# Sparse and linear attention on one core: three reciprocals on ScalarE, GpSimd masks in two steps, a hand-written ending per engine

## The chip, the cores and the metric

The kernel runs on one core of one Trainium2 chip. The metric is the device time of one launch, in microseconds (us). A core has five engines that run their own instruction streams and wait for each other by semaphores: TensorE (PE), VectorE (DVE), ScalarE (ACT), GpSimd (POOL) and SyncE (SP), which here only issues DMAs.

## The reference, cut to what matters

32 batches of 256 tokens with 128 channels, 16 heads of 8 channels. For each batch and head, scores of 256 x 256 are made, the 12 largest of each row are kept (`topk = int(256 * 0.05)`), and a sparse softmax over them is mixed with a linear attention over all keys:

```python
def _L0_attn_ref(x, Wqkv, bqkv, q_gamma, q_beta, k_gamma, k_beta, alpha, Wproj, bproj):
    ...
    q = _layernorm(q, q_gamma, q_beta)
    k = _layernorm(k, k_gamma, k_beta)
    scores = jnp.einsum('bhnd,bhmd->bhnm', q, k) / jnp.sqrt(jnp.float32(D))
    aw = jax.nn.softmax(scores, axis=-1)
    topk = max(1, int(N * TOPK_RATIO))
    kth = jax.lax.top_k(aw, topk)[0][..., -1:]
    mask = (aw >= kth).astype(aw.dtype)
    aws = aw * mask
    aws = aws / (aws.sum(-1, keepdims=True) + 1e-08)
    o_s = jnp.einsum('bhnm,bhmd->bhnd', aws, v)
    qf = jax.nn.softmax(q, axis=-1)
    kf = jax.nn.softmax(k, axis=-1)
    kv = jnp.einsum('bhnd,bhne->bhde', kf, v)
    z = jnp.einsum('bhnd,bhd->bhn', qf, kf.sum(axis=2))
    o_l = jnp.einsum('bhnd,bhde->bhne', qf, kv) / (z[..., None] + 1e-06)
    o = (a * o_s + (1.0 - a) * o_l).transpose(0, 2, 1, 3).reshape(B, N, C)
    return o @ Wproj.T + bproj
    ...
xn = _layernorm(x, axis=-1)
x = x + _L0_attn_ref(xn, ...) + _L0_ffn_ref(xn, ...)
```

The second branch picks one of eight 128 x 128 matrices and applies it to `xn`.

## The kernel before

A batch is cut into 8 units (`UNITS`) of two heads. A unit has four tiles (`TILES`) of 128 queries x 256 keys. All engines run `body(it)` for `it` from -2 to B + 1; in an iteration each engine steps through the units `u_` = 0 to 7, in an order written out by hand, and the batches are staggered: scores of batch `it`, input and normalisation of batches `it + 1` and `it + 2`, output of `it - 1` and `it - 2`. No scheduler is involved.

A tile goes this way. PE makes the scores (`score_ps`, two buffers). DVE takes the 8 largest (`largest`, tile `top`). POOL subtracts the row maximum (`drop`). ACT takes the exponential (`e`, with the row sum in `z`) and that of the 8 largest (`e8`). One unit later DVE removes those 8 (`remove`, MATCH_REPLACE8, tile `rest`) and takes the next 8 (`following`, tile `next`), of which one is the twelfth largest value, the threshold. Two units after the scores the mask `below` is made: POOL compares 24 of a batch's 32 tiles with the threshold (`POOL_TILES` tiles of each unit), ACT makes the other 8 with a Relu of the difference. Four units after the scores PE transposes `e` and adds the mask times -2^40 (`turn`, into `turn_ps`), ACT clips that to `kept` with a Relu, and PE multiplies it with the values (`product`, one quad of four heads at a time, into `pv_ps`). ACT copies each quad to `oT`, PE turns the four quads back with a transpose against `gather` (`sums`), and ACT copies numerators and denominators to `sums_sb`.

Three sets of reciprocals are taken on DVE, each of 128 x 32 numbers, once a batch, inside `extra`: `lin_z` (denominator of the linear attention) in unit 4, `k_rec` (softmax of k) in unit 6, and `den` (denominator of the sparse attention, to which POOL first adds 1e-8 times `z` in two instructions) in unit 7. POOL then multiplies by them (`lin`, `k_feat`, `o_sparse`). ACT normalises the input (`xn`, two instructions of 128 x 128 in unit 5). The output of a batch is put together in `early` of units 1 and 3, two iterations later: transposes of `o_sparse` and `lin`, an ACT copy `osT`, then the residual `x_res`, the chosen matrix, a bias and the projection. The last two batches go through the same code, in iterations 32 and 33, where most branches are empty.

## Time and profile before

| | us |
|---|---|
| median of three runs | 1214.25 (1212.27 to 1215.47) |
| the profiled execution, its own time | 1203.79 |
| its span, first to last instruction | 1202.0 |
| busy in the span | PE 951.5, DVE 1164.2, ACT 1094.4, POOL 1090.9 |

Busy time of an engine is the union of its instructions, so two that overlap count once. "Mean ns" is the duration of one instruction; since neighbours overlap, the step from one start to the next is often shorter. "idle before" is the gap in front of an instruction, and behind the arrow stands who ended it.

### The profile page before, as it was taken

Reading aid. Unit: us, or ns where it says so; the run is one execution under the profiler, and the core shown is the slowest. Engines: PE = TensorE matmul, PEld = TensorE weight load, DVE = VectorE, ACT = ScalarE, POOL = GpSimd, SP = SyncE. Lnnn points to the kernel's source line nnn. Section 1 sums busy time; section 2 is a strip of 40 time slices with the busy share of each in tenths; the row PEclk is TensorE's granted clock in tenths of the full one; section 3 lists DMA queues with packets and bytes.
Section 4 is the critical chain, followed back from the end, with each engine's and each line's share of the span. In section 5 each row is a group of like instructions: output and inputs, shape, how many; then the busy total and the mean of one; then the engine's idle time right before and its main releaser. Section 6 shows DMA issues by size and latency. Waiting matters only on the chain.

```text
span 1202.0 us, 34514 instructions
## 1 busy us (share of the span) xinstructions
PE 951.5 (79%) x9028; PEld 647.2 (54%) x9028; DVE 1164.2 (97%) x4448; ACT 1094.4 (91%) x3566; POOL 1090.9 (91%) x1691
## 2 busy tenths in 40 slices
PE   4578788887788788788788787888888788787786
PEld 1355555555555555555555555555555555555554
DVE  6999999999999999999999999999999999999993
ACT  3699999999999999999999998999999999999984
POOL 5699999999999999999999999999999999999974
PEclk9999999999999999999999999999999999999998
DMA  3122222122222122222122222122222121222210
GB/s 102 41 63 67 86 84 72 49 70 65 85 85 80 42 75 59 85 85 85 38 74 59 85 85 84 40 73 59 85 85 85 46 67 58 85 81 80 58 34 14
DMA packets 165126, 82.77 MB, mean 69 GB/s; under 512 B 7737, under 2 KB 164927, under 8 KB 164930
## 3 DMA queue, kind: packets, MB, share of 16 engines
q1 hardware_dynamic: 164658, 80.43, 23.4%
q8 instruction: 74, 1.21, 0.4%
q14 instruction: 122, 1.00, 0.3%
q10 hardware_dynamic: 272, 0.13, 0.0%
HBM read 42.78 MB, written 37.75 MB: 67 GB/s over the span
## 4 chain that ended last, share of the span: by engine, by line
ACT 33%; DVE 28%; issue 19%; PE 9%; POOL 8%; DVEq 2%; DMA 0%; POOLq 0%; ACTq 0%
ACT e L821 19%; DVE rest L646 11%; DVE top L639 10%; POOL below L440 6%; ACT kept L788 4%; DVE next L652 4%; PE pv_ps L964 3%; PE work_ps L1030 2%; ACT below L834 2%; DVEq L75 2%; ACT e L826 1%; PE turn_ps L943 1%; ACT osT L793 1%; ACT oT L843 1%; ACT xnT L882 1%
## 5 line engine op out<-in xcount | busy, mean ns | idle before, releaser
L440 POOL TENSOR_SCALAR below<-e,next 128x256 bf16<-128x256 f32 x768 | 695.8, 922 | 0.0
L821 ACT ACTIVATE e<-score_ps,drop 128x256 f32<-128x256 f32 x1024 | 475.1, 493 | 42.8 <-POOL drop L410 39.7
L646 DVE MATCH_REPLACE8 rest<-e 128x256 f32<-128x256 f32 x1024 | 416.7, 411 | 0.1
L652 DVE MAX8 next<-rest 128x8 f32<-128x256 f32 x1024 | 409.4, 413 | 0.3
L943 PE MATMUL turn_ps<-ident,e 128*128 128x128 f32 x2048 | 388.4, 284 | 15.7 <-ACT kept L788 15.7
L944 PE MATMUL turn_ps<-minus_huge,below 128*128 128x128 bf16 x2048 | 367.8, 221 | 0.0
L639 DVE MAX8 top<-score_ps 128x8 f32<-128x256 f32 x1024 | 361.0, 417 | 3.3 <-PE score_ps L925 3.1
L943 PEld LDWEIGHTS turn_ps<-ident,e 128*128 128x128 f32 x2048 | 290.7, 142 | 67.2 <-issue 33.1
L788 ACT ACTIVATE kept<-turn_ps 128x1024 f32<-128x1024 f32 x256 | 272.1, 1063 | 23.3 <-PE turn_ps L944 23.1
L821 ACT ACTIVATION_READ_ACCUMULATOR e<-score_ps,drop 128x1 f32 x1024 | 230.9, 226 | 0.0
L944 PEld LDWEIGHTS turn_ps<-minus_huge,below 128*128 128x128 bf16 x2048 | 218.6, 107 | 0.7
L964 PE MATMUL pv_ps<-kept,v_aug 128*32 128x256 f32 x2048 | 138.1, 387 | 58.0 <-ACT sums_sb L850 56.8
L834 ACT ACTIVATE below<-e,next 128x256 bf16<-128x256 f32 x256 | 128.8, 532 | 0.0
L925 PE MATMUL score_ps<-k_slots,q_slots 64*128 64x256 bf16 x1024 | 103.0, 278 | 13.4 <-issue 7.2
L964 PEld LDWEIGHTS pv_ps<-kept,v_aug 128*32 128x32 f32 x2048 | 56.3, 109 | 100.3 <-issue 80.2
L410 POOL TENSOR_TENSOR drop<-top 128x36 f32<-128x36 f32 x256 | 62.8, 245 | 47.8 <-DVE top L639 45.1
L646 DVE MATCH_VALUE_LOAD rest<-e 128x8 f32 x1024 | 79.2, 77 | 2.3 <-ACT e L826 0.6
L925 PEld LDWEIGHTS score_ps<-k_slots,q_slots 64*128 64x128 bf16 x1024 | 30.7, 94 | 72.0 <-issue 64.5
L826 ACT ACTIVATE e<-drop 128x32 f32<-128x32 f32 x256 | 66.7, 261 | 0.0
L1042 PE MATMUL work_ps<-w_qk,xnT 128*128 128x256 f32 x128 | 46.8, 449 | 20.0 <-ACT xnT L882 20.0
L1063 PE MATMUL work_ps<-kv,qfT 128*128 128x144 f32 x128 | 25.4, 323 | 43.6 <-DVE kv L660 43.6
L843 ACT COPY oT<-pv_ps 128x256 f32<-128x256 f32 x128 | 52.3, 409 | 1.3 <-PE pv_ps L964 1.3
(176 smaller groups left out, 1346.2 us busy)
## 6 DMA issues: line engine op xcount, KB each, us to landing
part_slots<-part SPq DMA_DIRECT2D x128, 192.0 KB, 2.3
q_slots<-part_slots SPq DMA_DIRECT2D x64, 256.0 KB, 3.5
k_slots<-part_slots SPq DMA_DIRECT2D x64, 256.0 KB, 3.9
part_slots<-part SPq DMA_DIRECT2D x64, 128.0 KB, 1.9
x_sb<-in_L_attn_x SPq DMA_DIRECT2D x32, 128.0 KB, 4.1
x_res<-in_L_attn_x SPq DMA_DIRECT2D x32, 128.0 KB, 4.1
out_y<-out_sb SPq DMA_DIRECT2D x32, 128.0 KB, 4.3
w_ops<-in_L_ffn_W SPq DMA_DIRECT2D x1, 512.0 KB
```

What stands on the lines that cost most here:

```text
L440: nc.gpsimd.tensor_scalar(below[:, r, t, :], e[:, r, t, :], next8[:, r, t, TOPK - 9:TOPK - 8], None, ALU.is_lt).then_inc(s["below_pool"], 1)
L639: nc.vector.max(top[:, q, t, 1:9], score_ps[:, q, t // 2, t % 2, :]).then_inc(s["top_ready"], 1)
L646: nc.vector.match_replace(rest[:, t, :], e8[:, (u_ - 1) % 2, t, :], e[:, (u_ - 1) % RING, t, :], REMOVED).then_inc(s["rest_ready"], 1)
L652: nc.vector.max(next8[:, (u_ - 1) % RING, t, :], rest[:, t, :]).then_inc(s["next_ready"], 1)
L788: nc.scalar.activation(kept[:, u_ % 4], turn_ps[:], ACT.Relu).then_inc(s["turn_copied"], 1)
L821: nc.scalar.activation(e[:, u_ % RING, t, :], score_ps[:, u_ % 2, t // 2, t % 2, :], ACT.Exp, bias=drop[:, u_ % 2, t, 0:1], accum_out=z[:, ...
L826: nc.scalar.activation(e8[:, u_ % 2], drop[:, u_ % 2, :, 1:9], ACT.Exp).then_inc(s["e8_ready"], 1)
L834: nc.scalar.activation(below[:, r, t, :], e[:, r, t, :], ACT.Relu, scale=-1.0, bias=next8[:, r, t, TOPK - 9:TOPK - 8]).then_inc(s["below_a ...
L925: last = mm(score_ps[:, v_ % 2, hh, nt, :], q_slots[rows, side, v_, nt * P:(nt + 1) * P], k_slots[rows, side, v_, :], start=True, stop=True)
L943: mm(dst, e[:, r, t, keys], ident[:], start=True, stop=False, is_transpose=True)
L944: last = mm(dst, below[:, r, t, keys], minus_huge[:], start=False, stop=True)
L964: last = mm(pv_ps[32 * j:32 * (j + 1), 0:N], v_aug[:, side, mc, 4 * q + j, :], kept[:, v_ % 4, j % 2, mc, :], start=(mc == 0), stop=(mc == ...
```

## The change

- **Reciprocals.** `sums_sb`, `lin_raw` and `k_sum` become three parts of one tile `over`. DVE's three reciprocals are gone. ACT takes one logarithm of the 128 x 96 denominators in unit 6 and one exponential of minus that in unit 7 (`over_log`, `over_rec`). They serve `k_feat` of batch `it + 1`, `lin` of `it` and `o_sparse` of `it - 1`. `lin` moves on POOL from unit 4 to unit 0 of the next iteration. POOL's two instructions for 1e-8 times `z` are gone; PE adds it with two matmuls against `eps_ident`.
- **Masks.** POOL first makes `gap` = threshold - e in bf16, one TENSOR_SCALAR (multiply by -1, add the threshold) for each tile, waits for them, and then clips all tiles of the unit in one TENSOR_SCALAR (min 2^40, max 0) to `below`. POOL makes 25 tiles of a batch, ACT 7.
- **Input.** `xn` goes from ACT (unit 5) to POOL (unit 4), two TENSOR_SCALAR with two pointer operands.
- **Copies.** `pv_ps` is used in halves, so ACT copies two quads at once (512 columns) in units 0 and 4, twice a batch where it was four times. `sums` multiplies by a `gather` of 36 columns, where it transposed against 128. `x_res` and `out_sb` are doubled; `x_res` is loaded at the end of SP's `body(it)` without a wait.
- **Ending.** Iterations 32 and 33 are gone. Each engine has its own ending: the residual, matrix and bias of the last two batches are accumulated in `work_ps` ahead of it; units 4 to 7 of the last batch are turned alternately into `turn_ps` and `score_ps`; DVE makes two masks, clips two halves of `kept`, and takes the last reciprocal and product straight from PSUM. In the diff `end_tile` turns one tile, `end_kept` is the Relu to `kept`, `end_product` one quad, `end_turned` two transposes, `end_out` the projection, `end_osT` and `end_y` the copies to `osT` and `out_sb`.

```diff
-POOL_TILES = (3, 2, 4, 3, 4, 3, 3, 2)
+POOL_TILES = (3, 3, 3, 3, 4, 3, 3, 3)
...
-        lin_z = sb("lin_z", [P, NT * H])
+        over = sb("over", [P, 3 * NT * H, VA])
+        over_log = sb("over_log", [P, 3 * NT * H])
+        over_rec = sb("over_rec", [P, 3 * NT * H])
+        sums_sb, lin_raw = over[:, 0:NT * H], over[:, NT * H:2 * NT * H]
+        k_sum = over[:, 2 * NT * H:, D]
+        sums_rec, lin_rec, k_rec = (over_rec[:, i * NT * H:(i + 1) * NT * H] for i in range(3))
...
-            for it in range(-2, B + 2):
+            for it in range(-2, B):
...
+                if exists(it):
+                    sp.dma_start(x_res[:, par], x_t[it]).then_inc(res_loaded[par], 16)
...
-                        nc.gpsimd.tensor_scalar(den[:, 0], z[:, nxt].rearrange("p t h -> p (t h)"), SUM_EPS, None,
-                                                ALU.mult).then_inc(s["den_step"], 1)
-                        pool.wait_ge(s["den_step"], it)
-                        nc.gpsimd.tensor_tensor(den[:, 1], den[:, 0], sums_sb[:, :, D], ALU.add).then_inc(
-                            s["den_ready"], 1)
...
-                        for t in range(POOL_TILES[r]):
-                            wait_alone(pool, s["next_ready"], TILES * (g - 2) + t + 1, s["waits_passed"])
-                            nc.gpsimd.tensor_scalar(below[:, r, t, :], e[:, r, t, :],
-                                                    next8[:, r, t, TOPK - 9:TOPK - 8], None,
-                                                    ALU.is_lt).then_inc(s["below_pool"], 1)
+                        half, many = u_ % 2, POOL_TILES[r]
+                        for t in range(many):
+                            pool.wait_ge(s["next_ready"], TILES * (g - 2) + t + 1)
+                            nc.gpsimd.tensor_scalar(gap[:, half, t, :], e[:, r, t, :], -1.0,
+                                                    next8[:, r, t, TOPK - 9:TOPK - 8], ALU.mult,
+                                                    ALU.add).then_inc(s["gap_step"], 1)
+                        pool.wait_ge(s["gap_step"], POOL_SUM * ((g - 2) // UNITS) + POOL_UPTO[r + 1])
+                        nc.gpsimd.tensor_scalar(below[:, r, 0:many], gap[:, half, 0:many], HUGE, 0.0, ALU.min,
+                                                ALU.max).then_inc(s["below_pool"], many)
...
+                    if u_ == 0 and exists(it - 1):
...
+                        pool.wait_ge(s["over_ready"], it + 1)
+                        nc.gpsimd.tensor_tensor(lin[:, nxt].rearrange("p t (h d) -> p (t h) d", d=D),
+                                                lin_raw[:, :, 0:D],
+                                                lin_rec.unsqueeze(2).to_broadcast([P, NT * H, D]),
+                                                ALU.mult).then_inc(s["lin_ready"], 1)
...
+                        wait(pool, s["w_xT"], it + 3)
+                        for t in range(NT):
+                            nc.gpsimd.tensor_scalar(xn[:, t], x_sb[:, par, t], rsqrt[:, 3, GROUPS + t:GROUPS + t + 1],
+                                                    x_shift[:, 1, t:t + 1], ALU.mult, ALU.add).then_inc(s["xn_ready"], 1)
...
+            for u_ in (UNITS - 2, UNITS - 1):
+                for t in range(2):
+                    wait_alone(pool, s["next_ready"], TILES * ((B - 1) * UNITS + u_) + t + 1, s["waits_passed"])
+                    nc.gpsimd.tensor_scalar(below[:, u_, t, :], e[:, u_, t, :], next8[:, u_, t, TOPK - 9:TOPK - 8],
+                                            None, ALU.is_lt).then_inc(s["below_pool"], 1)
...
-                    if u_ == 4 and k == 1 and exists(it):
-                        dve.wait_ge(s["lin_copied"], it + 1)
-                        nc.vector.reciprocal(lin_z[:], lin_raw[:, :, D]).then_inc(s["linz_ready"], 1)
-                    if u_ == 7 and k == 1 and exists(it - 1):
-                        dve.wait_ge(s["den_ready"], it)
-                        nc.vector.reciprocal(den[:, 2], den[:, 1]).then_inc(s["rden_ready"], 1)
...
-                    if u_ == 6 and exists(it + 1) and k == 5:
-                        dve.wait_ge(s["ksum_ready"], it + 2)
-                        nc.vector.reciprocal(k_rec[:], k_sum[:]).then_inc(s["krec_ready"], 1)
...
+                nc.vector.tensor_scalar(below[:, UNITS - 1, t, :], e[:, UNITS - 1, t, :],
+                                        next8[:, UNITS - 1, t, TOPK - 9:TOPK - 8], None,
+                                        ALU.is_lt).then_inc(s["below_dve"], 1)
+            for u_ in (2, 3):
+                src = (turn_ps, score_ps[:, 0])[u_ - 2]
+                dve.wait_ge(s["pv_ready"], QUADS * B - 2)
+                dve.wait_ge(s["half_ready"], u_ - 1)
+                nc.vector.tensor_scalar(kept[:, u_, 1], src[:, 1], 0.0, None, ALU.max).then_inc(s["half_copied"], 1)
...
+            dve.wait_ge(s["w_turn"], B)
+            dve.wait_ge(s["osp_ready"], B - 1)
+            nc.vector.reciprocal(sums_rec, sums[:, :, D]).then_inc(s["over_ready"], 1)
...
+            nc.vector.tensor_tensor(o_sparse[:].rearrange("p t (h d) -> p (t h) d", d=D), sums[:, :, 0:D],
+                                    sums_rec.unsqueeze(2).to_broadcast([P, NT * H, D]),
+                                    ALU.mult).then_inc(s["osp_ready"], 1)
...
+                    if u_ == 7 and it >= -1 and (exists(it + 1) or exists(it) or exists(it - 1)):
...
+                        act.wait_ge(s["over_logs"], it + 2)
+                        lo, hi = over_range(it)
+                        nc.scalar.activation(over_rec[:, lo:hi], over_log[:, lo:hi], ACT.Exp, scale=-1.0).then_inc(
+                            s["over_ready"], 1)
...
-                    if u_ % 2 == 0 and exists(it if u_ >= 6 else it - 1):
+                    if u_ in (0, 4) and exists(it - 1):
...
-                        nc.scalar.copy(oT[:, par if u_ >= 6 else nxt, (u_ - 6) // 2 % 4], pv_ps[:, 0:N]).then_inc(
+                        if u_ == 0:
+                            wait(act, s["w_turn"], it - 2)
+                        nc.scalar.copy(oT[:, nxt, u_ // 4].rearrange("p a n -> p (a n)"), pv_ps[:]).then_inc(
                             s["pv_copied"], 1)
...
+                    if u_ == 5 and it == -2:
...
+                    if u_ == 6 and it >= -1 and (exists(it + 1) or exists(it) or exists(it - 1)):
+                        if exists(it + 1):
+                            act.wait_ge(s["ksum_ready"], it + 2)
+                        if exists(it):
+                            act.wait_ge(s["lin_copied"], it + 1)
...
+                        lo, hi = over_range(it)
+                        nc.scalar.activation(over_log[:, lo:hi], over[:, lo:hi, D], ACT.Ln).then_inc(
+                            s["over_logs"], 1)
...
+            end_kept(0, kept[:, 0], turn_ps[:])
+            act.wait_ge(s["next_ready"], TILES * (B * UNITS - 1))
+            for t in (2, 3):
+                nc.scalar.activation(below[:, UNITS - 2, t, :], e[:, UNITS - 2, t, :], ACT.Relu, scale=-1.0,
+                                     bias=next8[:, UNITS - 2, t, TOPK - 9:TOPK - 8]).then_inc(s["below_act"], 1)
+            end_kept(1, kept[:, 1], score_ps[:, 0])
+            end_kept(2, kept[:, 2, 0], turn_ps[:, 0])
+            end_osT(B - 2, score_ps[:, 1, 0].rearrange("p t n -> p (t n)")[:, 0:N])
+            act.wait_ge(s["pv_ready"], QUADS * B - 2)
+            nc.scalar.copy(oT[:, side, 0].rearrange("p a n -> p (a n)"), pv_ps[:]).then_inc(s["pv_copied"], 1)
+            end_kept(3, kept[:, 3, 0], score_ps[:, 0, 0])
+            act.wait_ge(s["pv_ready"], QUADS * B - 1)
+            nc.scalar.copy(oT[:, side, 1, 1], pv_ps[:, N:2 * N]).then_inc(s["pv_copied"], 1)
+            act.wait_ge(s["pv_ready"], QUADS * B)
+            nc.scalar.copy(oT[:, side, 1, 0], score_ps[:, 1, 1, 0, :]).then_inc(s["pv_copied"], 1)
+            end_y(B - 2)
+            end_osT(B - 1, turn_ps[:, 1].rearrange("p m n -> p (m n)")[:, 0:N])
+            end_y(B - 1)
...
-                            last = nc.tensor.transpose(pv_ps[:, at:at + P], oT[:, nxt, q, t * P:(t + 1) * P], gather[:])
+                            mm(pv_ps[:, at:at + 4 * VA], oT[:, nxt, q // 2, 1 - q % 2, t * P:(t + 1) * P], gather[:],
+                               start=(t == 0 and q == 0), stop=False, skip_group_check=True)
...
+                    for t in range(NT):
+                        over_t = pv_ps[:, t * H * VA:(t + 1) * H * VA].rearrange("p (h e) -> p h e", e=VA)[:, :, D]
+                        last = mm(over_t, eps_ident[:], z[:, nxt, t, :], start=False, stop=True, skip_group_check=True)
                     last.then_inc(s["w_turn"], 1)
...
+                    if (it, u_) == (B - 1, 5):
...
+                                at = (b - B + 2) * NT * C + t * C
+                                dst = work_ps[:, at:at + C]
+                                mm(dst, ident[:], x_res[:, b % 2, t, :], start=(b == B - 2 and t == 0), stop=False,
+                                   skip_group_check=True)
+                                mm(dst, xnT[:, b % XRING, t * P:(t + 1) * P], w_sel[:], start=False, stop=False,
+                                   skip_group_check=True)
+                                mm(dst, ones3[:], bias3[:, 3 * C:4 * C], start=False, stop=False, skip_group_check=True)
...
+                if u_ == 2:
+                    pe.wait_ge(s["below_act"], act_done + 2)
+                end_tile(r, 0, dst)
+                end_tile(r, 1, dst).then_inc(s["turn_ready"], 1)
+                if u_ == 3:
+                    pe.wait_ge(s["below_dve"], 1)
+                end_tile(r, 2, dst)
+                if u_ == 3:
+                    pe.wait_ge(s["below_dve"], 2)
+                end_tile(r, 3, dst).then_inc(s["half_ready"], 1)
...
+            end_product(2, pv_ps[:, N:2 * N], range(4)).then_inc(s["pv_ready"], 1)
+            pe.wait_ge(s["half_copied"], 1)
+            end_product(3, score_ps[:, 1, 1, 0, :], (0, 1))
+            pe.wait_ge(s["turn_copied"], UNITS * B)
+            pe.wait_ge(s["half_copied"], 2)
+            end_product(3, score_ps[:, 1, 1, 0, :], (2, 3)).then_inc(s["pv_ready"], 1)
...
+                    at = (t * QUADS + q) * 4 * VA
+                    last = mm(sums_ps[:, at:at + 4 * VA], oT[:, side, q // 2, 1 - q % 2, t * P:(t + 1) * P], gather[:],
+                              start=False, stop=(q == QUADS - 1), skip_group_check=True)
+            last.then_inc(s["w_turn"], 1)
+            end_out(B - 2)
...
+            pe.wait_ge(s["lin_ready"], B)
+            end_turned(new, lin[:, side], True)
+            pe.wait_ge(s["osp_ready"], B)
+            end_turned(new, o_sparse, False).then_inc(s["w_osT"], 1)
+            pe.wait_ge(s["y_ready"], B - 1)
+            end_out(B - 1)
```

The first place is POOL in units 4 and 5 in the middle of the run. Before:

```order
L410 TENSOR_TENSOR drop<-top 128x36 [waits top_ready,e8_ready]
L440 TENSOR_SCALAR below<-e,next 128x256 [waits next_ready] x4
L342 TENSOR_TENSOR x_shift<-moments,rsqrt 128x2 [waits newton]
L345 TENSOR_SCALAR x_shift<-x_shift 128x2 [waits newton]
L457 TENSOR_TENSOR lin<-lin_raw,lin_z 128x256 [waits linz_ready]
L410 TENSOR_TENSOR drop<-top 128x36 [waits top_ready,e8_ready]
L440 TENSOR_SCALAR below<-e,next 128x256 [waits next_ready] x3
```

The same place now:

```order
L412 TENSOR_TENSOR drop<-top 128x36 [waits top_ready,e8_ready]
L343 TENSOR_TENSOR x_shift<-moments,rsqrt 128x2 [waits newton]
L346 TENSOR_SCALAR x_shift<-x_shift 128x2 [waits newton]
L437 TENSOR_SCALAR gap<-e,next 128x256 [waits next_ready] x3
L441 TENSOR_SCALAR below<-gap 128x768 [waits gap_step]
L464 TENSOR_SCALAR xn<-x_sb,rsqrt,x_shift 128x128 [waits w_xT,newton]
L464 TENSOR_SCALAR xn<-x_sb,rsqrt,x_shift 128x128
L412 TENSOR_TENSOR drop<-top 128x36 [waits top_ready,e8_ready]
L437 TENSOR_SCALAR gap<-e,next 128x256 [waits next_ready] x3
L441 TENSOR_SCALAR below<-gap 128x768 [waits gap_step]
```

`xn` now stands in front of the `drop` of unit 5, where `lin` stood; the comparison of each tile has become a pass for each tile and one for the unit; the unit has three POOL tiles where it had four.

The second place is DVE in unit 4, from its two first removals. Before:

```order
L646 MATCH_REPLACE rest<-e 128x256 [waits e8_ready,next_ready] x2
L670 RECIPROCAL lin_z<-lin_raw 128x32 [waits lin_copied]
L652 MAX next<-rest 128x8 [waits rest_ready]
L646 MATCH_REPLACE rest<-e 128x256 [waits e8_ready,next_ready]
L652 MAX next<-rest 128x8 [waits rest_ready]
```

And now:

```order
L661 MATCH_REPLACE rest<-e 128x256 [waits e8_ready,next_ready] x2
L667 MAX next<-rest 128x8 [waits rest_ready]
L661 MATCH_REPLACE rest<-e 128x256 [waits e8_ready,next_ready]
L667 MAX next<-rest 128x8 [waits rest_ready]
L661 MATCH_REPLACE rest<-e 128x256 [waits e8_ready,next_ready]
```

Only the reciprocal is gone; units 6 and 7 read likewise.

The third place is the end of DVE's stream. Before:

```order
L646 MATCH_REPLACE rest<-e 128x256 [waits e8_ready,next_ready] x2
L652 MAX next<-rest 128x8 [waits rest_ready]
L646 MATCH_REPLACE rest<-e 128x256 [waits e8_ready,next_ready]
L652 MAX next<-rest 128x8 [waits rest_ready]
L646 MATCH_REPLACE rest<-e 128x256 [waits e8_ready,next_ready]
L652 MAX next<-rest 128x8 [waits rest_ready] x2
L674 RECIPROCAL den<-den 128x32 [waits den_ready]
```

And now:

```order
L748 MAX next<-rest 128x8 [waits rest_ready]
L742 MATCH_REPLACE rest<-e 128x256 [waits e8_ready,next_ready]
L748 MAX next<-rest 128x8 [waits rest_ready] x2
L760 TENSOR_SCALAR below<-e,next 128x256 [waits next_ready] x2
L767 TENSOR_SCALAR kept<-turn_ps 128x512 [waits half_ready,pv_ready]
L767 TENSOR_SCALAR kept<-score_ps 128x512 [waits half_ready,pv_ready]
L771 RECIPROCAL over_rec<-turn_ps 128x32 [waits osp_ready,w_turn]
L774 TENSOR_TENSOR o_sparse<-turn_ps,over_rec 128x256 [waits over_ready,w_osT]
```

Behind its last maximum DVE has six more instructions where it had one.

## Rows read from the trace of the kernel before

**Rows 1.** Chain of work in the middle: start, us, what, count.

```profile
407.88 1.40 DVE top L639 x4
...
443.62 1.40 DVE top L639 x4
```

**Rows 2.** Windows: busy (instructions) of PE, PEld, DVE, ACT, POOL; PEclk, DMA share, GB/s.

```profile
407.88:443.62 35.74, 29.05 (x285) 19.89 (x284) 35.68 (x138) 34.00 (x112) 33.81 (x53) 1.00 0.25 71
...
1180.00:1202.00 22.00, 14.31 (x118) 10.46 (x116) 1.40 (x4) 6.34 (x12) 4.71 (x7) 0.83 0.07 19
```

**Rows 3.** DVE timeline, unit 4 with a reciprocal, unit 5 without; group of one.

```profile
624.52 0.41 DVE L646 MATCH_REPLACE8 rest<-e 128x256 f32<-128x256 f32 x1
624.85 0.35 DVE L670 RECIPROCAL lin_z<-lin_raw 128x32 f32<-128x32 f32 x1
...
625.39 0.07 DVE L646 MATCH_VALUE_LOAD rest<-e 128x8 f32 x1
...
628.93 0.42 DVE L646 MATCH_REPLACE8 rest<-e 128x256 f32<-128x256 f32 x1
...
629.59 0.08 DVE L646 MATCH_VALUE_LOAD rest<-e 128x8 f32 x1
...
L670 DVE RECIPROCAL lin_z<-lin_raw 128x32 f32<-128x32 f32 x32 | 11.1, 346 | 0.0
```

**Rows 4.** POOL's groups by shape: busy us, mean ns, idle before.

```profile
L440 POOL TENSOR_SCALAR below<-e,next 128x256 bf16<-128x256 f32 x768 | 695.8, 922 | 0.0
...
L426 POOL TENSOR_SCALAR den<-z 128x32 f32<-128x32 f32 x32 | 9.6, 301 | 11.6 <-ACT sums_sb L850 8.9
...
L334 POOL TENSOR_SCALAR rsqrt<-rsqrt 128x66 f32<-128x66 f32 x30 | 7.7, 256 | 6.0 <-POOL rsqrt L332 6.0
...
L345 POOL TENSOR_SCALAR x_shift<-x_shift 128x2 f32<-128x2 f32 x31 | 7.0, 227 | 6.2 <-POOL x_shift L342 6.2
...
L391 POOL TENSOR_SCALAR bias_rest<-bias_rest,ident 3x128 f32<-3x128 f32 x1 | 0.6, 593 | 0.0
```

**Rows 5.** POOL's waits from 194 to 1140 us: in total, times, longest.

```profile
POOL drop L410 <- DVE top L639: 23.1, 61, 1.0
```

**Rows 6.** ACT's groups by shape, same columns as rows 4.

```profile
L834 ACT ACTIVATE below<-e,next 128x256 bf16<-128x256 f32 x256 | 128.8, 532 | 0.0
...
L843 ACT COPY oT<-pv_ps 128x256 f32<-128x256 f32 x128 | 52.3, 409 | 1.3 <-PE pv_ps L964 1.3
...
L878 ACT ACTIVATE xn<-x_sb,x_shift,rsqrt 128x128 f32<-128x128 f32 x64 | 29.0, 519 | 2.0 <-DVE x_shift L543 2.0
...
L766 ACT ACTIVATE log<-moments 128x66 f32<-128x66 f32 x31 | 12.5, 404 | 0.6 <-DVE moments L569 0.6
```

**Rows 7.** Timelines of POOL, PE, ACT and DVE, units 5 to 7.

```profile
629.34 0.24 POOL L410 TENSOR_TENSOR drop<-top 128x36 f32<-128x36 f32 x1
...
632.49 1.07 PE L964 MATMUL pv_ps<-kept,v_aug 128*32 128x256 f32 x16 [1.88 <-ACT sums_sb L850]
...
636.82 0.25 ACT L826 ACTIVATE e<-drop 128x32 f32<-128x32 f32 x1
...
637.24 0.09 DVE L646 MATCH_VALUE_LOAD rest<-e 128x8 f32 x1
```

**Rows 8.** Timelines of the end.

```profile
1180.30 0.75 DVE L652 MAX8 next<-rest 128x8 f32<-128x256 f32 x2
...
1179.02 4.51 POOL L440 TENSOR_SCALAR below<-e,next 128x256 bf16<-128x256 f32 x5
...
1189.13 1.07 PE L964 MATMUL pv_ps<-kept,v_aug 128*32 128x256 f32 x16 [0.55 <-ACT out_sb L870]
...
1199.35 0.37 ACT L870 COPY out_sb<-pv_ps 128x256 f32<-128x256 f32 x1 [4.04 <-PE pv_ps L1017]
```

**Rows 9.** Timelines of PE and DVE at the first scores.

```profile
30.14 0.61 PE L925 MATMUL score_ps<-k_slots,q_slots 64*128 64x256 bf16 x4
...
31.45 1.43 DVE L639 MAX8 top<-score_ps 128x8 f32<-128x256 f32 x4
```

217 lines of the change are left out of this document (160 added, 57 removed).

## Prediction

> **What bounds the kernel now.** I read the chain of work first, to find the period: the four maxima of the same unit start at 407.88 and again at 443.62 [rows 1], so a batch takes 35.74 us, and 32 batches make nearly the whole span. Then the windows over just that stretch [rows 2]: DVE is busy 35.68 of 35.74 us, ACT 34.00, POOL 33.81, PE 29.05. DVE has no gap; it is the bound. But ACT and POOL are only 5% below it, so whatever DVE gives up is worth its full price only if both of them get cheaper or stay within the new period. Last the end [rows 2, 8]: DVE's last maximum ends at 1181.05 (1180.30 + 0.75) and the span at 1202.0. In the last 22 us DVE is busy 1.4, ACT 6.3, POOL 4.7: 21.0 us of mere latency, at a mean granted PE clock of 0.83.
>
> The sum is made against the profiled execution, 1203.79 us with a span of 1202.0. The median of the runs is 1214.25, 10.5 above it; nothing in the trace says where that lies, so I take it as a constant and put the saving on the median.
>
> **DVE's three reciprocals.** One lasts 346 ns, but DVE overlaps neighbours, so I take starts. With a reciprocal, from a MATCH_REPLACE8 to the load that follows the next maximum: 624.52 to 625.39, 0.87 us. Without: 628.93 to 629.59, 0.66 us [rows 3]. One costs 0.21 us. There are 32 of each of three; the first `k_rec` lies in the start and the last `den` in the ending, so 94 lie in the saturated stream: 94 x 0.21 = **19.7 us**. Nothing is added to DVE in the steady part. Its floor is then 35.74 - 0.63 = 35.11 us a batch.
>
> **Can POOL follow.** POOL's work apart from masks: 33.81 - 24 x 0.906 (695.8 / 768) [rows 2, 4] = 12.1 us. It idles 1.93 a batch, of which 0.87 is waiting for DVE (23.1 us in 946 us, that is 26.5 batches) [rows 5]; the other 1.06 are waits on its own results, so 13.1 is fixed. Off: the scaling of `z`, 0.30 [rows 4], and an addition about as long, 0.6. On: `xn`, two TENSOR_SCALAR of 128 columns, between 0.26 (66 columns, two steps) and 0.59 (128 columns, one step, pointer) [rows 4]; I take 0.4, so 0.8. Fixed is then 13.3, and the masks may take 35.11 - 13.3 = **21.8 us** a batch before POOL decides. They take 21.7 now.
>
> The new masks are not in the trace, so I bound them from its TENSOR_SCALAR rows [rows 4]. The one-step ones lie on a line: 2 columns 227 ns, 32 columns 301, 128 with a pointer 593, 256 with a pointer 922; about 2.5 ns a column. The only two-step one (multiply, then add, `rsqrt`) has 66 columns and takes 256 ns, where that line gives 385. So it costs at most (256 - 227) / 64 = 0.45 ns a column: the two-step form is several times faster a column. Both new passes are of that form. A `gap` pass: 0.227 + 0.06 for the pointer + 254 x 0.00045 = 0.40 us at the low end, 0.92 at the one-step line. The clip of 768 columns: 0.57, or 2.12; of 1024: 0.69, or 2.75. A batch has 25 gaps, seven clips of 768, one of 1024, and eight waits for its own result of 0.2 (6.0 us in 30) [rows 4]. Low end 10.0 + 4.7 + 1.6 = 16.3 us; high end 23.0 + 17.6 + 1.6 = 42.2. I take a value near the low end, 16 to 20, because the nearest row in form is the two-step one; pointer, bf16 and min/max are what it does not show. POOL then needs 30 to 33 us a batch and is under the floor.
>
> GPSIMD Engine Reference, section 3.1, of the Trainium skill gives 1.03 cycles an element at 1.2 GHz for a loop of at most two operations, bound by its ports, and section 7 gives a compare loop twice that when it is not unrolled. Comparing rows agree in direction (the compare is slow), not in size, since 922 ns is 2.5 ns a column. By 0.86 ns an element the 12,800 columns of both passes would be an estimated 11 us, with fixed parts and waits 21.6 us a batch: under 21.8, so the sum would be the same, with no slack.
>
> **Can ACT follow.** Off [rows 6]: two `xn` of 519 ns, one mask of 532. On: a logarithm and an exponential of 96 columns, each near the 404 ns of 66. Four `oT` copies of 409 ns become two of twice the width, worth nothing if the width is all that costs. 34.00 - 1.04 - 0.53 + 0.81 = 33.2 us, under 35.11. The logarithm waits for `k_sum`, which POOL makes a unit earlier; behind it on ACT stand the copy `xnT` and the next `kept`, so a late POOL would reach PE and DVE by it. The thin place is units 5 to 7 [rows 7]: `drop` at 629.34, from it ACT, then PE's product that waits for `sums_sb`, then `e8` done at 637.07, and DVE needs it at 637.24. The margin is 0.17, and one reciprocal less in between takes 0.21. It holds only if `drop` comes earlier. In front of it POOL now has three cheap tiles and `xn` (2.0 + 0.8) in place of four tiles and `lin` (about 4.2), so it does. PE does less than before and is busy 29.05; I cost its edits at nothing, and the second `x_res` too, since it is loaded a batch and more ahead.
>
> **The start.** The first maximum waits for DVE's setup at 31.45, with scores there by 30.75 [rows 9]. DVE no longer stands waiting for `k_sum` before that setup, so PE sets the time: **0.4 us**.
>
> **The ending.** From the last maximum: two masks 0.7; PE turns the last tile 0.4, but POOL's last masks (after the batch's `o_sparse`, at 1179.02 and then four of 0.9) [rows 8] come 1.6 after the maximum, and PE has two units to turn after them: PE is through some 3 us after the maximum. Then quads 2 and 3, 1.07 each [rows 8]; `oT` 0.4; `sums` 0.3; reciprocal and product 0.8; transposes 0.5; `osT` 0.4; projection 0.7; copy 0.37; and from its end to the span's end 2.3 as now (1199.72 to 1202.0) [rows 8]. That is 10.9, with hops not yet in it about 12. Bounds: 10 if POOL is early, 14 if the low PE clock stretches it. 21.0 - 12 = **9.0 us**, 7 to 11.
>
> Sum: 19.7 + 0.4 + 9.0 = 29.1. Profiled span 1173, median 1214.25 - 29.1 = **1185 us**.
>
> **The rivals.**
> - *The gain is real, but POOL or the unit 5 to 7 chain takes part of it* (17%). The masks cost 22 to 24 us a batch, or `drop` stays late, so that a period of 35.3 to 35.6 is reached. Per tile that is 0.9 us or more with waits. For it: everything but the masks already fills 13.3 us, and units are uneven (units 1 and 3 get a tile more, unit 0 gets `lin`). Gain: 4 to 14 steady + 9.4: 1191 to 1201.
> - *One of the two passes costs what a one-step pass costs* (12%). Slow gaps: 23.0 + 4.7 + 1.6 = 29.3; slow clips: 10.0 + 17.6 + 1.6 = 29.2. POOL needs 42.6 us a batch and becomes the bound: 32 x (42.6 - 35.74) = +220, less the ending: about 1425, slower. Masks of 22.4 us a batch undo the steady gain, and from 22.7 on the whole is slower. For it: no row has a two-step pass with a pointer or a bf16 input. Against it: the pointer costs 0.06 in the one-step rows.
> - *The change does not do what it says* (3%): DVE loses its reciprocals, and waits for PE or ACT as long. For it: three engines lie within 6% of the period [rows 2], so 0.63 us is soon lost at another one. Then only the ending counts, and if it too is eaten, 1214; within 0.3%.
> - The forecast as described: 68%, its own range 1178 to 1192.
>
> **How the numbers follow.** 0.3% (3.6 us) is about what a measurement of this kernel can tell from no change. Faster: 68 + 17 = 85%; same 3%; slower 12%. The range must leave out no more than 2 in 10: it leaves out the slower case, no change, and a little on each side, so it runs from 1176 (ending 11, some idle gone) to 1201.
>
> **What would show it.** Steps of 35.1 between the unit's maxima, DVE still without gaps; two-step rows at 0.4 to 0.5 us for 256 columns and 0.6 to 0.9 for 768; POOL busy 29 to 32 a batch; ACT near 33; 10 to 14 us from the last maximum to the end. The prediction is wrong if DVE waits for `e8` or for scores in unit 7, if ACT waits for `drop` more than now, or if `gap` takes 0.9 us.

## The result, and the profile after

The changed kernel takes 1222.93 us (median of 8 runs, 1216.61 to 1226.95), beside 1213.09 us for the kernel before: a ratio of 1.0074, 95% interval 1.0049 to 1.0100. It is slower by 0.7%, where I had forecast 1185 us. Its profiled execution took 1222.3 us, with a span of 1220.5.

The page of the changed kernel, its busy times and the granted PE clock in 40 slices:

```profile
PE 1011.5 (83%) x9381; PEld 707.2 (58%) x9412; DVE 1151.5 (94%) x4358; ACT 1065.0 (87%) x3474; POOL 995.2 (82%) x1972
...
PEclk9989999999999899999999999899999999999988
```

The mean granted clock is 0.962; the profiled execution before had 0.990. That execution was not a usual one: in 79 more runs of the kernel before, taken beside the experiments, the clock is 0.968 in the median (0.952 to 0.984), so none came up to 0.990. Over whole runs the two kernels' clocks are near each other (0.968 and 0.962). PE is the only engine whose busy time grew. The windows of the changed kernel show one batch without and one with a fall of the clock, then three stretches inside the second (columns as in [rows 2]):

```profile
261.33:296.78 35.45, 30.00 (x293) 21.35 (x294) 35.09 (x136) 33.02 (x109) 30.91 (x62) 1.00 0.25 72
296.78:333.49 36.71, 31.42 (x293) 21.99 (x294) 35.20 (x136) 33.13 (x108) 30.62 (x62) 0.95 0.24 70
308.89:311.50 2.61, 2.61 (x21) 2.32 (x21) 2.61 (x12) 2.61 (x7) 2.43 (x6) 0.97 0.45 132
311.50:314.90 3.40, 3.40 (x25) 2.23 (x28) 3.40 (x14) 2.38 (x10) 2.75 (x7) 0.52 0.09 24
```

The first batch is what I had forecast, all but 0.34 us: DVE busy 35.09 (forecast 35.11), ACT 33.02 (33.2), POOL 30.91 (30 to 33). The second is 1.26 us longer, and what differs is the clock: 3.4 us at about 1.2 GHz, right behind the sums. I count a batch by DVE's `kv`, from one to the next, and look at windows of 1 us. In the profiled execution before, the steps were 35.75 us in most batches, and none had a fall between 12 and 17.5 us behind `kv`. Now 17 of 31 have one there, and their steps are 36.8 in the median; the 12 batches without any fall have 35.6 in the median, most often 35.45. The timeline of the changed kernel's PE through that place:

```profile
308.89 1.98 PE L1084 MATMUL pv_ps<-gather,oT 128*128 128x36 f32 x16 [1.07 <-ACT oT L901]
310.70 0.60 PE L1090 MATMUL pv_ps<-z,eps_ident 128*128 128x16 f32 x4
311.14 0.43 PE L1097 MATMUL work_ps<-part,minus_one 128*128 128x512 bf16 x1
311.51 0.61 PE L1033 MATMUL score_ps<-k_slots,q_slots 64*128 64x256 bf16 x4
312.05 0.47 PE L1051 MATMUL turn_ps<-ident,e 128*128 128x128 f32 x1
```

The sums were 8 transposes. They are now 16 passes of 36 columns and 4 of 16 columns. (A plain f32 product shows two matmul records, a transpose or a bf16 product one; each record is called a pass here.) Behind them the turn of the unit's four tiles runs at half clock, ACT gets `kept` late, PE's next scores are late, and DVE waits. DVE's waits in the changed kernel (us in total, times, longest):

```profile
DVE top L654 <- PE score_ps L1033: 34.1, 33, 5.5
DVE rest L661 <- ACT e L884: 15.4, 31, 0.6
```

The first line was 3.1 us before and the second 0.6. The longest case of the first is in the last batch, where the ending lays the residual and feed-forward passes of two batches in front of unit 6's turn. They take 5.46 us at clock 0.50:

```profile
1189.22:1194.68 5.46, 5.46 (x22) 4.10 (x20) 4.92 (x19) 1.06 (x5) 3.69 (x7) 0.50 0.00 0
```

```profile
1199.67 1.43 DVE L654 MAX8 top<-score_ps 128x8 f32<-128x256 f32 x4 [5.52 <-PE score_ps L1033]
...
1206.81 0.74 DVE L748 MAX8 next<-rest 128x8 f32<-128x256 f32 x2
...
1214.23 0.36 DVE L771 RECIPROCAL over_rec<-turn_ps 128x32 f32<-128x32 f32 x1 [3.59 <-PE turn_ps L1329]
```

The ending itself, from the last maximum (1206.81 + 0.74) to 1220.5, is 13.0 us, where it was 21.0 [rows 8].

### The profile page after: what moved, and what is told of

The parts are those of the page before. It is cut to its first block, busy times and chain, and to the rows that moved or that the text cites. A ratio compares the mean times of both kernels' runs of the same rounds, so it can differ in the third digit from the quotient of the medians.

```text
span 1220.5 us, 34803 instructions
## 1 busy us (share of the span) xinstructions
PE 1011.5 (83%) x9381; PEld 707.2 (58%) x9412; DVE 1151.5 (94%) x4358; ACT 1065.0 (87%) x3474; POOL 995.2 (82%) x1972
## 3 DMA queue, kind: packets, MB, share of 16 engines
q8 instruction: 77, 1.26, 0.4%
## 4 chain that ended last, share of the span: by engine, by line
POOL 32%; PE 27%; ACT 19%; issue 15%; DVE 5%; DMA 1%; DVEq 0%; POOLq 0%; ACTq 0%; SPq 0%
ACT e L879 12%; POOL gap L437 10%; POOL below L441 5%; PE turn_ps L1051 5%; PE pv_ps L1073 3%; POOL qkn L359 3%; PE work_ps L1156 3%; POOL qk_b L359 3%; PE pv_ps L1084 3%; DVE top L654 3%; PE turn_ps L1052 2%; POOL drop L412 2%; PE work_ps L1144 2%; PE work_ps L1187 2%; POOL sq_half L422 2%
## 5 line engine op out<-in xcount | busy, mean ns | idle before, releaser
L1051 PE MATMUL turn_ps<-ident,e 128*128 128x128 f32 x2016 | 401.9, 293 | 21.0 <-ACT part L863 17.5
L1052 PE MATMUL turn_ps<-minus_huge,below 128*128 128x128 bf16 x2016 | 380.0, 226 | 0.0
L437 POOL TENSOR_SCALAR gap<-e,next 128x256 bf16<-128x256 f32 x794 | 368.9, 479 | 0.0
L1051 PEld LDWEIGHTS turn_ps<-ident,e 128*128 128x128 f32 x2016 | 296.8, 147 | 59.3 <-issue 21.7
L839 ACT ACTIVATE kept<-turn_ps 128x1024 f32<-128x1024 f32 x252 | 267.5, 1062 | 56.9 <-PE turn_ps L1052 56.9
L441 POOL TENSOR_SCALAR below<-gap 128x768 bf16<-128x768 bf16 (+1 forms) x254 | 216.7, 853 | 41.4 <-POOL gap L437 41.4
L1073 PE MATMUL pv_ps<-kept,v_aug 128*32 128x256 f32 x2000 | 142.2, 404 | 2.9 <-ACT over L908 2.2
L892 ACT ACTIVATE below<-e,next 128x256 bf16<-128x256 f32 x222 | 120.1, 541 | 0.0
L1084 PE MATMUL pv_ps<-gather,oT 128*128 128x36 f32 x496 | 61.7, 281 | 32.8 <-ACT oT L901 32.8
L1084 PEld LDWEIGHTS pv_ps<-gather,oT 128*128 128x128 f32 x496 | 58.1, 192 | 39.8 <-ACT oT L901 39.8
```

The lines of the kernel that those rows point to most:

```text
L437: nc.gpsimd.tensor_scalar(gap[:, half, t, :], e[:, r, t, :], -1.0, next8[:, r, t, TOPK - 9:TOPK - 8], ALU.mult, ALU.add).then_inc(s["gap_s ...
L441: nc.gpsimd.tensor_scalar(below[:, r, 0:many], gap[:, half, 0:many], HUGE, 0.0, ALU.min, ALU.max).then_inc(s["below_pool"], many)
L839: nc.scalar.activation(kept[:, u_ % 4], turn_ps[:], ACT.Relu).then_inc(s["turn_copied"], 1)
L1051: mm(dst, e[:, r, t, keys], ident[:], start=True, stop=False, is_transpose=True)
L1052: last = mm(dst, below[:, r, t, keys], minus_huge[:], start=False, stop=True)
L1073: last = mm(pv_ps[32 * j:32 * (j + 1), half * N:(half + 1) * N], v_aug[:, side, mc, 4 * q + j, :], kept[:, v_ % 4, j % 2, mc, :], start=(m ...
```

## The experiments

Every ratio is to the kernel before, run on the same chip in the same rounds. "Dips" are batches, of 31 in the profiled execution, in which a 1 us window 12 to 17.5 us behind `kv` has a granted clock under 0.9. "Spread" says that the ending's output passes are issued in four parts, in units 4 to 7 of the last batch.

My first theory was that the longer sums leave PE too much work without a gap, that the chip lowers the clock for it, and DVE then waits. A first rival was that the longer sums delay product and `e8` at full clock too; a second, that the packing of PE as a whole is at fault.

**Sums by transposes.** In this build each transpose opens the bank anew, so the 1e-8 z passes replace sums instead of adding to them; the work is the same.

```
-   gather = sb("gather", [P, 4 * VA])
+   gather = sb("gather", [P, P])
...
-   mm(pv_ps[:, at:at + 4 * VA], oT[:, nxt, q // 2, 1 - q % 2, t * P:(t + 1) * P], gather[:],
-      start=(t == 0 and q == 0), stop=False, skip_group_check=True)
+   last = nc.tensor.transpose(pv_ps[:, at:at + P],
+                              oT[:, nxt, q // 2, 1 - q % 2, t * P:(t + 1) * P], gather[:])
```

> The changed kernel, with one part undone: the sums of a batch are gathered by 8 transposes as before, instead of 16 plain f32 passes; the 4 passes that add 1e-8 z stay. Theory 1 (the extra passes fill PE's last idle time in unit 5, its granted clock then falls to 1.2 GHz there in most batches, and DVE waits for turns and scores of unit 6): the batches of 36 to 37 us mostly become 35.45, mean clock 0.98 or more, 1192 to 1200 us. Theory 2 (the clock is not what costs; the longer sums stand in the chain sums, copy, product, e8): every batch gains up to 0.9 us, those at full clock too, so that steps under 35.3 appear. Theory 3 (PE's packing as a whole, by faster masks and wider oT copies, not the sums): 1218 to 1224 us, clock still near 0.962.

Measured: 1195.54 us, ratio 0.9849 (0.9822 to 0.9877), no dips, most steps 35.50. The sums' form is worth 27 us, as my first theory said (1192 to 1200). Full-clock steps did not get shorter, which is against the first rival. Then the same without the four passes:

```
-   for t in range(NT):
-       over_t = pv_ps[:, t * H * VA:(t + 1) * H * VA].rearrange("p (h e) -> p h e", e=VA)[:, :, D]
-       last = mm(over_t, eps_ident[:], z[:, nxt, t, :], start=False, stop=True, skip_group_check=True)
```

> The same with the 4 passes that add 1e-8 z to the sums left out too (outside the ending), so PE has in unit 5 what it had before the change; the term 1e-8 z is missing. Theory 1: as good as the transposes alone or 1 to 5 us better, 1188 to 1198 us, with dips of the clock as rare as before (some 4 of 31 batches over 36 us). Theory 2: 0.3 us a batch, 10 us, below the run with transposes alone. Theory 3: 1216 to 1224 us.

Measured: 1200.28 us, 0.9893 (0.9870 to 0.9916), 1 dip, steps of 35.51. Less PE work brought nothing, so the 0.60 us of the four passes is not on the path here. Why it came out 5 us above the run before, with 4 falls of the clock 21 to 30 us in, I did not settle.

**Plain sums alone, in the kernel before.**

```
-   last = nc.tensor.transpose(pv_ps[:, at:at + P], oT[:, nxt, q, t * P:(t + 1) * P], gather[:])
+   last = mm(pv_ps[:, at:at + 4 * VA], oT[:, nxt, q, t * P:(t + 1) * P], gather[:, 0:4 * VA],
+             start=(t == 0 and q == 0), stop=(t == NT - 1 and q == QUADS - 1), skip_group_check=True)
```

> The kernel before, with only the sums changed: 16 plain f32 passes of 36 columns in place of 8 transposes (no 1e-8 z passes on PE). It adds about 0.9 us of PE's time in unit 5 and nothing elsewhere. Theory 1: clock falls in most batches, 20 to 30 batches of 36 us or more, 1225 to 1240 us, mean clock under 0.975. Theory 2: the sums are 0.9 later for ACT and for PE's product in every batch, steps of about 36.5 at full clock, 1235 to 1242 us. Theory 3: no change, 1211 to 1217 us.

Measured: 1209.46 us, 0.9963 (0.9943 to 0.9983), 5 dips. All three missed. Five dips come where the profiled execution before had none, but a batch with one takes 36.0 where the others take 35.78. PE still waits for `sums_sb` there (35.1 us in 30 waits), and I think that this slack takes up the low clock; no run shows it by itself. The run also says something against a simple rule. Over its 12 runs the clock is 0.975 to 0.988, where the kernel before had 0.952 to 0.983 in the same rounds, and it is 0.4% faster. So in that schedule the 36-column passes did not lower the clock of the whole run but went with a higher one. What they do in the changed kernel hangs on what stands around them, and what that is stays open.

**The ending's passes spread.**

```
-   if (it, u_) == (B - 1, 5):
-       for b in (B - 2, B - 1):
-           for t in range(NT):
+   if it == B - 1 and u_ >= 4:
+       b, t = B - 2 + (u_ - 4) // 2, u_ % 2
```

> The changed kernel, with the 20 passes that lay residual, feed-forward and bias of the last two batches into the output tile ahead of time issued in four parts in units 4 to 7 of the last batch, instead of all in unit 5. In the changed kernel they take 5.5 us at half clock, and DVE's maxima of unit 7 wait 5.52 us behind them. If the block as such is the cause: that wait falls under 1.5 us and the time by 4 to 5 us, to about 1218. If the wait comes from elsewhere (the low clock of all of the last batch): at most 1 us faster.

Measured: 1221.69 us, 1.0056 (1.0033 to 1.0079); from the last `kv` to the end 39.1 us in the profiled execution (45.6 without the change), and the 5.52 us wait is gone. I had expected 1218; the median does not show the gain (1.2 us below the changed kernel, inside both intervals), and its profiled execution has 20 dips. In the run with transposes and the unspread block, DVE waited only 0.17 us there, with the clock at 1.00. So the block costs 5 us only when it meets the low clock, as far as one execution of each shows.

**Both repairs together.** Only the first transpose clears the bank, so the four passes add.

```
+   mm(pv_ps[:, at:at + P], oT[:, nxt, q // 2, 1 - q % 2, t * P:(t + 1) * P], gather[:],
+      start=(t == 0 and q == 0), stop=False, is_transpose=True, skip_group_check=True)
```

> The changed kernel with both repairs together: sums by 8 transposes (the first alone clears the bank, the others add onto it, so that the 1e-8 z passes add onto the sums), and the output's passes of the last two batches spread over units 4 to 7. Theory 1 (clock): as the run with transposes alone, 1195.5, less the 4 to 6 us of the unit 7 wait: 1189 to 1193 us, both kernels beaten. If the spread passes give their gain back elsewhere in the ending: 1195 to 1198.

Measured: 1196.52 us, 0.9864 (0.9836 to 0.9892), no dips. It beats both kernels, the one before by 1.4%. The clock of its six runs is 0.981 to 0.991; with plain sums and the same ending it was 0.959 to 0.969 in twelve. Its windows for one batch, and DVE's waits:

```profile
617.38:652.89 35.51, 29.04 (x285) 20.33 (x286) 35.06 (x136) 33.08 (x108) 30.98 (x62) 1.00 0.25 72
```

```profile
DVE rest L663 <- ACT e L886: 13.9, 32, 0.6
DVE top L656 <- PE score_ps L1035: 9.8, 12, 2.7
```

**Is it the amount of work?** The loop of 8 transposes is issued twice, on top of both repairs.

```
+   for t in range(NT):
+       for q in range(QUADS):
+           at = (t * QUADS + q) * 4 * VA
+           mm(pv_ps[:, at:at + P], oT[:, nxt, q // 2, 1 - q % 2, t * P:(t + 1) * P], gather[:],
+              start=(t == 0 and q == 0), stop=False, is_transpose=True, skip_group_check=True)
```

> The kernel of the run before this in the list, with the loop of 8 transposes issued twice (the second set rewrites the first), so that unit 5 again holds as much PE work as with the plain passes, 2.2 us of sums, but in the form that did not disturb. Theory 1 as I hold it now (what counts is that PE has work without a gap there, not which form it has): dips of the clock 14 us into the batch are back in 12 or more of 31 batches, 1205 to 1220 us. Rival (the plain f32 form is what draws the clock down, not the length): no more dips than with one set, within 4 us of it. Rival (longer sums delay product and e8 at full clock): steps without a dip rise from 35.50 by 0.5 or more.

Measured: 1196.90 us, 0.9859 (0.9830 to 0.9888), no dips. My first theory falls here. In its windows, PE is as busy as in the changed kernel, with as many records (21 in 2.32 us), and the 3.4 us behind stay at 1.00:

```profile
307.30:309.62 2.32, 2.32 (x21) 2.24 (x21) 2.32 (x10) 2.32 (x6) 2.32 (x6) 1.00 0.35 101
309.62:313.00 3.38, 3.11 (x38) 1.94 (x37) 3.38 (x14) 3.38 (x12) 2.62 (x8) 1.00 0.16 49
```

**Plain sums without the four passes.** The edit of the second experiment, on the changed kernel with the spread ending.

> The changed kernel with its 16 plain passes and the spread output passes, but without the 4 passes that add 1e-8 z (that term is left out outside the ending), which takes 0.60 us of PE's unit 5 away. With plain passes and the 4 it took 1221.7 with 17 dips 13 to 15 us into the batch; the kernel before with plain passes and no such term had 6. Theory 1: 5 to 12 such dips, 1197 to 1212 us. If the four passes are nothing to it: 16 or more dips and 1217 to 1223.

Measured: 1210.67 us, 0.9968 (0.9947 to 0.9989), 17 dips. The dips are as many as the second expectation said, the time is as the first said: they cost less without the four passes (median step 36.5).

**Is POOL late?** On top of both repairs, `xn` goes back to ACT:

```
-   if u_ == 5 and it == -2:
+   if u_ == 5 and exists(it + 2):
...
-   nc.gpsimd.tensor_scalar(xn[:, t], x_sb[:, par, t], rsqrt[:, 3, GROUPS + t:GROUPS + t + 1],
-                           x_shift[:, 1, t:t + 1], ALU.mult, ALU.add).then_inc(s["xn_ready"], 1)
```

> The first kernel of this list with the normalised input computed on ACT again, in unit 5 of every batch (two operations of 519 ns), and not on POOL (two TENSOR_SCALAR in front of unit 4's masks). It asks whether the 0.35 to 0.4 us by which a step without a dip (35.45 to 35.50) stays above 35.11 comes from POOL being late with drop in units 5 to 7. If so: steps fall to 35.2 to 35.4, the wait of DVE for e8 goes from about 0.5 to under 0.3 us a batch, 3 to 8 us faster. If ACT's own queue in units 5 to 7 is what makes e8 late: its 1.04 us more lengthen the steps to 35.7 or above, 8 to 25 us slower. Alike within 2 us if the two offset.

Measured: 1195.98 us, 0.9860 (0.9835 to 0.9885), steps of 35.50, DVE's wait for `e8` 15.6 us in all. Neither POOL nor ACT's load is seen to hold the step there; that two effects offset each other, which I had allowed for, this run cannot exclude.

**Is it the chain product, w_v, e8?** On top of both repairs, in unit 6 PE issues w_v and the scores first, then the product.

```
-   if u_ % 2 == 0 and exists(it if u_ >= 6 else it - 1):
+   if u_ in (0, 2, 4) and exists(it - 1):
        product(u_)
...
        scores(u_)
+   if u_ == 6 and exists(it):
+       product(u_)
```

> The changed kernel with both repairs (8 transposes, spread output passes; 1196.5 us), and in unit 6 PE issues the passes of w_v and the scores before the product that waits for ACT's copy of the sums, instead of behind it. In its trace of the kernel so far the only wait of DVE in a batch of 35.50 is 0.43 us for e8 in unit 7: ACT waits 0.99 us for w_v, which PE begins 1.07 us late, behind that product. Theory (this chain, not POOL, holds the step at 35.50): w_v comes about 0.6 us earlier, ACT's wait of 0.99 goes to 0.4 or less, DVE's wait goes, steps of 35.07 to 35.15, 12 to 13 us faster: 1183 to 1187 us. Rival (POOL's drop or ACT's queue is late next): 35.3 to 35.5, 1190 to 1197 us.

Measured: 1208.62 us, 0.9965 (0.9938 to 0.9992). The mechanism was right, the time wrong. DVE's wait for `e8` went from 13.9 to 2.5 us and steps of 35.0 to 35.1 appear, but the clock now falls 17 to 20.5 us in, in 12 batches. The windows of a batch without and one with it, and DVE's waits:

```profile
296.20:331.24 35.04, 28.95 (x285) 20.30 (x286) 35.04 (x136) 33.14 (x109) 30.91 (x62) 1.00 0.25 73
331.24:368.17 36.93, 30.38 (x285) 20.93 (x286) 35.06 (x136) 33.43 (x109) 30.94 (x62) 0.95 0.24 69
349.00:353.00 4.00, 4.00 (x31) 2.09 (x31) 4.00 (x16) 3.22 (x13) 2.91 (x7) 0.59 0.26 70
```

```profile
DVE top L656 <- PE score_ps L1035: 33.1, 23, 2.7
...
DVE rest L663 <- ACT e L886: 2.5, 10, 0.6
```

In the first, DVE is busy 35.04 of 35.04 us: this is the floor that I had forecast.

**Which form, which data?** On top of both repairs, the 16 plain passes stand in front of the 8 transposes, which overwrite them; in the second kernel they read zeros.

```
+   mm(pv_ps[:, at:at + 4 * VA], oT[:, nxt, q // 2, 1 - q % 2, t * P:(t + 1) * P], gather[:, 0:4 * VA],
+      start=(t == 0 and q == 0), stop=False, skip_group_check=True)
```

> The changed kernel with both repairs, and in front of the 8 transposes of each batch's sums also the 16 plain f32 passes of 36 columns, whose result the transposes overwrite. 8 further transposes in this place, about 1 us of PE, changed nothing (1196.9 us, no dip 14 us into the batch). If the plain f32 form is what goes with the fall of the clock: 12 or more dips 13 to 16 us into the batch, 1215 to 1235 us. If only the whole of PE's work without a gap counts, 1 us of work more is tolerated again and 2 us perhaps too: under 5 such dips, 1196 to 1202 us.

> The same, with the 16 plain f32 passes reading a tile of zeros for both operands. If the number of passes and weight loads alone goes with the dips: as many as with the real data, within 4, and the same time within 0.5%. If what the array computes (its switching) matters: at most half as many dips, and 1196 to 1210 us.

Measured: 1247.65 us, 1.0281 (1.0251 to 1.0311), 19 dips; with zeros 1246.99, 1.0272 (1.0242 to 1.0303), 24 dips. About 1 us more of transposes had cost nothing; 1.97 us more of 36-column passes cost 51 us, of which some 16 are length alone (steps without a fall are 36.03, not 35.50). The data make no difference to the time (the dips are 5 more, one more than I had allowed). Length is not yet separated from form here; the wide run below does that.

```
-   gather = sb("gather", [P, 4 * VA])
+   gather = sb("gather", [P, 4 * VA], BF16)
...
-   oT = sb("oT", [P, 2, QUADS // 2, 2, N])
+   oT = sb("oT", [P, 2, QUADS // 2, 2, N], BF16)
```

> The changed kernel with the output passes spread, and its sums plain as the change has them, but with oT and gather in bf16 (the attention's numerators and sums are rounded to bf16 there), so that each of the 8 products is one pass. The four passes that add 1e-8 z stay f32. If the f32 form is what goes with the dips: 0 to 5 of them 13 to 16 us into the batch, 1193 to 1199 us. If any product there that is no transpose does it: 12 or more and 1210 to 1222 us.

Measured: 1202.53 us, 0.9908 (0.9879 to 0.9938), 14 dips. It is not the f32 form: half as many passes, of 180 ns, come with nearly as many dips. The dips are cheaper (median step 36.2), perhaps because these sums end earlier.

```profile
L1084 PE MATMUL pv_ps<-gather,oT 128*128 128x36 bf16 x248 | 11.4, 180 | 33.0 <-ACT oT L901 33.0
```

**The place of the sums**, in the changed kernel with the spread ending.

```
-   if u_ == 5 and exists(it - 1):
-       sums()
    early(u_)
...
        scores(u_)
+   if u_ == 5 and exists(it - 1):
+       sums()
```

> The changed kernel with the output passes spread and the sums plain as in the change (16 passes and the 4 for 1e-8 z), but issued behind the scores of unit 5 instead of ahead of them. With the sums ahead of them it took 1221.7 us, with 17 or more dips 13 to 15 us into the batch. If their place ahead of the scores is what makes the dips costly: DVE's wait for scores falls from some 28 us to under 15, and 1198 to 1212 us, dips or not. If their presence in the batch decides: as many dips, a us or two later, and 1217 to 1225.

Measured: 1241.24 us, 1.0233 (1.0205 to 1.0261), 21 dips. As many dips as ahead of the scores, but dearer than either expectation: DVE's wait for scores is 48.5 us in all. Their place ahead of the scores is not what makes the dips. Then, on top of both repairs, only w_v ahead of the product:

```
    early(u_)
+   if u_ == 6 and exists(it):
+       product(u_)
```

> The changed kernel with both repairs (1196.5 us), and in unit 6 only w_v ahead of the product, the scores behind both as before (with both ahead of the product the steps without a dip were 35.07, but dips at 18 us and 26 us stood in 16 batches, 1208.6 us). If w_v alone cuts the chain: DVE's wait for e8 falls from 13.9 us to under 5, steps without a dip 35.1. If the dips come with any closing of PE's gap ahead of unit 7: 12 or more, 1203 to 1212 us; if they came from the product behind the scores alone: under 6, 1184 to 1190 us.

Measured: 1201.14 us, 0.9897 (0.9869 to 0.9924). DVE's wait for `e8` fell to 2.0 us and steps of 35.1 appear; 15 batches have a fall 17 to 20.5 us in. The timeline of PE shows what precedes one (the clock falls at 350):

```profile
345.21 0.40 PE L1035 MATMUL score_ps<-k_slots,q_slots 64*128 64x256 bf16 x4
...
348.64 0.49 PE L1146 MATMUL work_ps<-w_v,xnT 128*128 128x128 f32 x2 [1.46 <-ACT part L920]
...
349.79 1.49 PE L1075 MATMUL pv_ps<-kept,v_aug 128*32 128x256 f32 x16
```

This is a wait of PE and not a burst of work. That made a further theory, called theory 4 in the expectations: the clock falls where the array gets little, waits and short passes alike.

**Plain, but wide.** The same 16 plain f32 passes and the spread ending, with 128 columns a pass (the padded gather) instead of 36:

```
-   mm(pv_ps[:, at:at + 4 * VA], oT[:, nxt, q // 2, 1 - q % 2, t * P:(t + 1) * P], gather[:, 0:4 * VA],
+   mm(pv_ps[:, at:at + P], oT[:, nxt, q // 2, 1 - q % 2, t * P:(t + 1) * P], gather[:],
       start=(t == 0 and q == 0), stop=False, skip_group_check=True)
```

> The changed kernel with the output passes spread and its sums plain f32 products, but with the 128 columns of the padded gather instead of 36: the same 16 passes, each of 128 columns. The sums take 2 to 3 us of PE instead of 1.98. If the plain form draws the clock down (theory 1, too much to compute): 17 or more dips 12 to 17 us into the batch, more than with 36 columns, 1222 to 1235 us. If short passes are the trouble (theory 4: the chip lowers the clock where the array is given little between weight loads, though the trace shows PE busy): 0 to 5 dips there, 1194 to 1204 us.

Measured: 1195.76 us, 0.9844 (0.9818 to 0.9869), 1 dip. More work for the array, as many passes, as long in time, and 26 us less. Windows of one batch, of its sums, and of the stretch behind them:

```profile
259.02:294.47 35.45, 30.19 (x294) 21.31 (x294) 35.08 (x135) 33.03 (x108) 30.92 (x62) 1.00 0.25 72
306.57:309.14 2.57, 2.57 (x23) 2.34 (x23) 2.57 (x12) 2.57 (x7) 2.43 (x6) 1.00 0.43 122
309.14:312.50 3.36, 3.19 (x39) 2.16 (x38) 3.36 (x14) 3.34 (x11) 2.68 (x7) 1.00 0.12 31
```

```profile
306.57 2.05 PE L1086 MATMUL pv_ps<-gather,oT 128*128 128x128 f32 x16 [1.07 <-ACT oT L903]
```

The changed kernel had 2.61 us here and 0.52 behind them; in PE's program only the width of the 16 passes differs (and the ending's spread passes, which the 1221.7 us kernel has too). Its four runs have a clock of 0.987 to 0.993. This refutes the theory of too much work, and the transposing form isn't needed either. Next the bf16 kernel with the same widening:

> The kernel with oT and gather in bf16 (8 passes of 36 columns: 14 dips, 1202.5 us), with 128 columns a pass instead of 36; numerators and sums are rounded to bf16 as there. Theory 1: at least 14 dips. Theory 4 (short passes): 0 to 6 dips 12 to 17 us in, 1194 to 1200 us. Its whole work is half of the f32 form's, so some dips may stay.

Measured: 1197.58 us, 0.9850 (0.9826 to 0.9874), 12 dips. The time is as theory 4 said, the dips are not: they stay, at a lower price (35.8 to 36.2 us in most of these batches). So width alone does not keep the clock up where the passes are half as many: the clock of the runs rose from 0.958 to 0.969 only to 0.974 to 0.978. Theory 4 is no rule that these runs establish.

**The wait filled.** 16 bf16 passes of 128 columns that nothing reads, in front of w_v, in the two kernels that had w_v first.

```
+   if u_ == 6 and exists(it + 1) and exists(it):
+       wait_alone(pe, s["exp_done"], TILES * (it * UNITS + u_), s["waits_passed"])
+       for i in range(16):
+           mm(score_ps[:, 1, 0, 0, 0:P], minus_one[:], minus_one[:], start=True, stop=True)
```

> The kernel with both repairs and w_v ahead of the product in unit 6 (1201.1 us, 13 dips 17 to 19 us in), and in PE's wait ahead of w_v 16 bf16 passes of 128 columns into the bank of the next scores, which the scores overwrite; nothing reads them. About 0.9 us more work for PE, inside a wait of about 1 us. Theory 1 (PE has too much to do): more dips, 1203 us or above. Theory 4 (PE's idle time and short passes let the clock fall): under 6 dips at 17 to 19 us, steps of 35.1, 1184 to 1191 us, the forecast of 1185 nearly met.

> The same filling in the kernel with w_v and scores ahead of the product (1208.6 us, dips at 18 and 26 us in 16 batches). Theory 1: as many or more, 1208 us or above. Theory 4: the dips at 18 to 19 us go, those at 26 us may stay; 1185 to 1197 us.

Measured: 1202.38 us, 0.9889 (0.9860 to 0.9919), and 1202.37, 0.9886 (0.9855 to 0.9917). The falls at 17 to 20.5 us went from 15 batches to none, and from 12 to 1. So in these two kernels the falls there hang on PE's wait. The time did not follow in the first, which is as slow as unfilled: 6 batches now have a fall 21 to 30 us in, and DVE still waits 26.7 us for scores. The second gained 6 us on its unfilled form (0.8% by the ratios). That part of theory 4's forecast failed.

## Why the prediction was wrong, step by step

- **The step that failed: "PE does less than before and is busy 29.05; I cost its edits at nothing".** It does more: 30.00 us busy and 293 records from `kv` to `kv`, where it had 29.05 and 283 (the line below). The 0.95 us themselves cost nothing (35.45 with them, 35.50 without). What costs is their form in this schedule: the sums' transposes became 36-column passes, and with these the granted clock falls in 17 of 31 batches. With the same ending, plain sums take 1221.7 us, transposes 1196.5, plain sums of 128 columns 1195.8: **25 us**. It outweighs the whole steady gain of 19.7. In that sense the third rival happened, DVE waiting for PE instead, by a mechanism that I had not named. Why these passes bring the falls is not shown.

```profile
383.46:419.20 35.74, 29.05 (x283) 19.89 (x283) 35.67 (x138) 34.00 (x112) 33.82 (x52) 1.00 0.25 72
```

- **DVE's reciprocals, 19.7 us.** Right at the floor: 35.04 and 35.09 us busy, 35.11 forecast. As a step it is reached in full only where `e8` comes in time.
- **The thin place, units 5 to 7.** I named it, and gave it its relief by an earlier `drop`. The relief failed: DVE waits 0.43 us in each batch for `e8` ([rows 7] showed a margin of 0.17). Moving `xn` off POOL changed nothing; w_v ahead of the product took the wait away. The chain is ACT's copy of the sums, PE's product, w_v, ACT's `v_aug`, `e8`; no run shows POOL in it. It explains the 0.39 us by which an ordinary step stays above 35.11, or 12 us over 31 batches. That the repaired kernel's median stands just 11.5 us above 1185 is partly luck: its mean step in the profile is 35.84, since one batch with a fall takes 38.05 and others take 36.2 to 36.5 at full clock, where DVE waits 0.6 to 0.9 us for scores for a reason that I did not find.
- **The sum against one execution.** The profiled execution before has a mean step of 35.86 us, for it too has longer batches. Its span is 1202.0 us, that of the repaired kernel 1192.3, both at a clock of 0.990. Of these 9.7 us the 31 steps give 0.6, and the ending and the start nearly all. So between these two the 19.7 us of the steady part were not reached. The medians differ by 17 us. The runs' clocks differ too, 0.968 before and 0.988 repaired, and that may be where the rest comes from; no run shows it by itself.
- **POOL.** Right as a sum, at its upper end. A `gap` takes 479 ns, a clip of 768 columns 826, of 1024 1039, and with the waits the masks cost 19.7 us a batch (368.9 + 216.7 + 41.4 over 31.8 batches), 16 to 20 forecast. The clips' two sizes give 0.83 ns a column, where my low end had 0.45. The second rival, the slow pass, is out. The first was mis-stated: with 13.3 us fixed, masks of 22 to 24 us make a period of 35.3 to 37.3, not 35.3 to 35.6.

```profile
L437 POOL TENSOR_SCALAR gap<-e,next 128x256 bf16<-128x256 f32 x794 | 368.9, 479 | 0.0
L441 POOL TENSOR_SCALAR below<-gap 128x768 bf16<-128x768 bf16 x222 | 183.5, 826 | 36.0 <-POOL gap L437 36.0
L441 POOL TENSOR_SCALAR below<-gap 128x1024 bf16<-128x1024 bf16 x32 | 33.3, 1039 | 5.4 <-POOL gap L437 5.4
```

- **ACT** 33.02 (33.2), **the start** 0.46 (0.4; first `kv` at 42.08, before 42.54): right.
- **The ending, 9.0 us.** 8.0 from the last maximum. My "`sums` 0.3" was mis-sized: with the passes for 1e-8 `z` they take 2.4 us there, and DVE waits 3.59 for them. The passes laid ahead of time, which I did not cost at all, take back 5.5 us ahead of that maximum when the clock is low.

```profile
1211.77 0.62 PE L1324 MATMUL turn_ps<-z,eps_ident 128*128 128x16 f32 x4
1212.24 1.95 PE L1329 MATMUL turn_ps<-gather,oT 128*128 128x36 f32 x16
```

- **"Nothing in the trace says where" the 10.5 us between profile and median lie.** They are likely falls of the clock, which the profiled execution with its 0.990 had fewer of. Over the 79 runs of the kernel before, 0.01 less clock goes with 3.7 us more, and the line through them gives 1205.8 us at 0.990, beside 1203.8 measured. In the 8 runs of the changed kernel 0.01 goes with 9.2 us (1216.6 us at 0.967, 1226.95 at 0.956). So at nearly the same clock the low stretches cost the changed kernel more. Both are correlations over runs, not experiments. My constant assumed that the falls would stay as many and cost the same; the price did not stay.

TensorE: Matmul & The Clock Gate, Part 1, of the Trainium skill says that the low clock is the default and that activity of the engine releases it. The runs agree in direction where f32 passes were widened (1.00 behind them, 0.52 before) and where a wait was filled (15 batches to none). The profile's PE busy does not show this activity: it was 2.61 of 2.61 us ahead of the fall.

Open: transposes of 36 columns were not tried. The dips are counted in one profiled execution of each build; the clocks of the other runs bear out their order in the main. Also open is why the same plain sums went with a higher clock in the kernel before; why falls 21 to 30 us in became more frequent when those at 17 to 20.5 were filled away; and why each build has a few in places of their own. No build held 35.1 through all batches.

## What to carry to other kernels

When an edit exchanges PE instructions, count and compare their forms, and not only PE's busy share: equal time in narrower passes can go with a lower granted clock for the work behind, as in the changed kernel, and need not, as in the kernel before. Where PE has slack behind that place a fall may be nearly free (0.2 us a batch in the kernel before); a tightening elsewhere makes it cost. So read the granted clock along one batch, after every change on any engine, before explaining a wait by the engine that it names. And compare the clock of the profiled execution with that of the other runs before making a sum against it. A passage laid ahead of time is only free if nothing urgent stands behind it on its queue.

## What was not expected of the hardware

- 16 plain f32 passes took 1.98 us at 36 columns and 2.05 us at 128: the width hardly changed their time. Eight transposes of the same data took 1.09 us.

```profile
307.30 1.09 PE L1086 MATMUL pv_ps<-gather,oT 128*128 128x128 f32 x8 [1.08 <-ACT oT L903]
```

- The plain product shows twice as many matmul records as the transpose of the same operands (496 to 248 in 31 batches).
- Passes over a tile of zeros went with as low a clock as passes over data (0.945 to 0.957 and 0.945 to 0.951 over the runs; 1247.0 and 1247.7 us).
- GpSimd's two-step operation on 256 columns with a pointer took 479 ns, the one-step comparison 922 [rows 4].
